# Routed layers in one block: normalisation, gates and routing together, rows scattered in groups of four tiles into a fixed region for each expert

## The reference

```python
# pair 1: relu, no bias, an expert takes its first 320 tokens only
logits = tokens @ gate_w; probs = softmax(logits); expert_idx = argmax(probs)
mask1 = one_hot(expert_idx, E); pos = cumsum(mask1, axis=0) - 1
sec_mask = mask1[:, :, None] * one_hot(pos, 320)
h = relu(einsum('ecd,edf->ecf', expert_input, w1)); expert_output = einsum('ecf,efd->ecd', h, w2)
# pair 3: gelu, biases b1 and b2, no limit
h = gelu(x_flat @ w1[e] + b1[e]); y = h @ w2[e] + b2[e]
out = out + where(expert_idx == e, expert_w, 0)[:, None] * y
```

## Time and profile before

| | us |
|---|---|
| median of 3 runs | 3460.03 (3453.24 to 3462.03) |
| the profiled execution's own time | 3466.94 |
| its span in the profile | 3465.3 |
| TensorE busy | 2923.5 (84%) |
| POOL busy | 1298.7 (37%) |

### The profile page before, as it was taken

The page is one execution under the profiler, slowest core; times in us unless marked ns, Lnnn a source line. Parts: engine busy times, 40 slices in busy tenths (PEclk is TensorE's granted clock), DMA queues, the critical chain, the costliest instruction groups (busy, mean ns, idle before and its releaser), DMA issues. The chain is left out here.

```text
span 3465.3 us, 68349 instructions
## 1 busy us (share of the span) xinstructions
PE 2923.5 (84%) x26674; PEld 2032.6 (59%) x26675; DVE 2086.9 (60%) x3094; ACT 1894.2 (55%) x2864; POOL 1298.7 (37%) x941
## 2 busy tenths in 40 slices
PE   6679997735779998979998595979999999988596
PEld 3246665314436666536666595666666666657595
DVE  6968887485768774867783223756444444466222
ACT  3458885282448885548884111656555555456131
POOL 2259996020127885237873212630000000045212
PEclk9979998867889999989998798979999999989698
DMA  4511111100012220022222511011000000042612
GB/s 160 209 54 54 54 56 59 73 0 19 13 43 55 53 53 22 1 48 59 53 50 77 176 36 51 2 31 49 25 25 25 26 25 1 1 102 50 234 36 68
DMA packets 218052, 193.21 MB, mean 56 GB/s; under 512 B 126837, under 2 KB 176865, under 8 KB 216737
## 3 DMA queue, kind: packets, MB, share of 16 engines
q1 hardware_dynamic: 210247, 172.30, 17.2%
q0 software_dynamic: 5280, 14.42, 1.3%
q10 hardware_dynamic: 2233, 2.39, 0.2%
HBM read 112.72 MB, written 39.00 MB: 44 GB/s over the span
## 5 line engine op out<-in xcount | busy, mean ns | idle before, releaser
L2578 POOL TENSOR_TENSOR lta_p_lo<-lta_p,lta_p_hi 128x1024 f16<-128x1024 f32 x256 | 538.9, 2132 | 221.6 <-DVE lta_p_hi L2701 221.6
L2773 ACT ACTIVATE lta_p<-lta_banks,lt_gmax 128x512 f32<-128x512 f32 x512 | 323.7, 682 | 113.0 <-PE lta_banks L2616 108.5
L2684 DVE TENSOR_REDUCE lta_s_ps<-lta_s_ps 128x1 f32<-128x1101 f32 x240 | 314.2, 1309 | 106.8 <-PE lta_s_ps L2595 106.8
L3717 PE MATMUL m_h_ps<-m_x,m_w 128*128 128x512 f16 x1536 | 356.5, 383 | 4.1 <-issue 4.1
L3729 PE MATMUL m_y_ps<-m_w,m_hT 128*128 128x256 f16 x3072 | 355.8, 273 | 2.3 <-DVE m_hT L3887 2.3
L3887 DVE TENSOR_TENSOR m_hT<-m_h,m_hT 128x512 f16<-128x512 f32 x256 | 177.0, 692 | 281.1 <-ACT m_hT L3814 279.4
L3814 ACT ACTIVATE m_h<-m_h_ps,m_h_bias,m_h_scale 128x512 f32<-128x512 f32 x256 | 199.3, 778 | 266.0 <-PE m_h_ps L3717 257.8
L3729 PEld LDWEIGHTS m_y_ps<-m_w,m_hT 128*128 128x128 f16 x3072 | 298.9, 98 | 65.9 <-issue 8.6
L1227 POOL TENSOR_TENSOR c0a_tri_p_lo<-c0a_tri_p,c0a_tri_p_hi 128x1024 f16<-128x1024 f32 (+2 forms) x192 | 285.5, 1524 | 58.5 <-DVE c0a_tri_p_hi L1401 57.8
L3717 PEld LDWEIGHTS m_h_ps<-m_x,m_w 128*128 128x128 f16 x1536 | 151.1, 99 | 163.0 <-issue 10.6
L1476 ACT ACTIVATE c0a_tri_p<-c0a_banks,c_size 128x512 f32<-128x512 f32 (+3 forms) x384 | 208.3, 576 | 45.6 <-PE c0a_banks L1295 34.3
(11 more groups left out here) (758 smaller groups left out, 6574.7 us busy)
## 6 DMA issues: line engine op xcount, KB each, us to landing
m_w<-in_L_ffn_w_dram SPq DMA_DIRECT2D x4, 8192.0 KB, 39.0
m_raw<-in_L_ffn_W_dram SPq DMA_DIRECT2D x16, 1024.0 KB, 6.5
lta_q<-ltb_qT SPq DMA_DIRECT2D x96, 128.0 KB, 2.4
c_side<-in_fside_Bx16xSxS_dram SPq DMA_DIRECT2D x16, 616.0 KB, 4.9
c0a_tri_q<-c_near SPq DMA_DIRECT2D x96, 96.0 KB
c0a_tri_k<-c_mixed SPq DMA_DIRECT2D x93, 96.0 KB
lta_k<-ltb_kT SPq DMA_DIRECT2D x64, 137.6 KB, 2.5
lt_vh<-ltb_v SPq DMA_DIRECT2D x64, 128.0 KB
```

What stands on the lines that cost most here:

```text
L2578: nc.gpsimd.tensor_tensor(p_lo[:, slot, :], p32[:, p32_slot(h, j), :], p_hi[:, slot, :], ALU.subtract).then_inc(rested, 1)
L2684: nc.vector.tensor_reduce(ntop_of(h)[:, n:n + 1], scores(h, n), AX_X, ALU.max, negate=True).then_inc(top_ready, 1)
L2773: nc.scalar.activation(p32[0:rows, slot, c * 512:(c + 1) * 512], t_ps[0:rows, c, :], ACT.Exp, bias=bias, scale=p["gmax"][0:rows, 0:1]).the ...
L3717: last = nc.tensor.matmul(h_ps[:, f % RING, :], w1[:, v, a, c, f * P:(f + 1) * P], x16[:, b, c, n * CHUNK:(n + 1) * CHUNK], start=c == 0 a ...
```

## The change

- One block holds what were `layernorm_stage` and `route_tokens`. It works in four groups of four tiles: normalise two groups, then for each group choose the experts, normalise a later group, and compute the places. PE, ACT and DVE follow the same order by groups.
- A token's row in `sorted_x` no longer depends on how many tokens the other experts have: expert e owns the rows from e times 2048. So a group of tiles can be scattered as soon as it and the groups before it are counted; POOL waits for `slot_ready` once in four tiles. `sorted_x` grows from 2944 rows to 17408 (8 x 2048 + 8 x 128), 17.8 MB each.
- The old dense row is still computed, after the last group, for `sorted_y` and the gather. A new list `row_of` says for each of the 23 tiles at which row of `sorted_x` it begins; SP reads it with `value_load` before each of its loads.
- The zeros: SP's two fills in stage c0p go. Instead POOL issues four transfers of 4352 rows each at the end of its stream in `latent_project`, for `sorted_x0` in batch 0 and for `sorted_x1` in batch 1. They are waited for (`zero_stored`) before the scatter of the routed layer only.

```diff
@@ Env
-        self.sorted_x = [nc.dram_tensor(f"sorted_x{k}", [NT * P, D], F32).ap() for k in range(2)]
+        self.sorted_x = [nc.dram_tensor(f"sorted_x{k}", [SORTED_ROWS, D], F32).ap() for k in range(2)]
@@ stage c0p, sync
-        for rows, kept in zip(env.sorted_x, env.zero_stored):
-            sp.dma_start(rows.rearrange("(j p) d -> p j d", p=P),
-                         env.zero[:].unsqueeze(1).to_broadcast([P, NT, D])).then_inc(kept, 16)
@@ latent_project, gpsimd
         for n in range(LAST + 1):
             affine(n)
             rest(n)
+        rows = env.sorted_x[b].rearrange("(k j p) d -> k p j d", p=P, k=ZERO_FILLS)
+        for k in range(ZERO_FILLS):
+            nc.gpsimd.dma_start(rows[k], env.zero[:].unsqueeze(1).to_broadcast([P, SORTED_ROWS // P // ZERO_FILLS, D])
+                                ).then_inc(env.zero_stored[b], 16)
@@
+SORTED_ROWS = E * T + E * P
+ZERO_FILLS = 4
@@ route_tokens, gpsimd
-        pool.wait_ge(slot_ready, 1)
-        pool.wait_ge(zero_stored, 16)
+        pool.wait_ge(zero_stored, ZERO_FILLS * 16)
         for t in range(TILES):
-            nc.gpsimd.indirect_dma_start(sorted_x, bass.IndirectOffsetOnAxis(ap=slot[:, t:t + 1], axis=0),
+            if t % GROUP == 0:
+                pool.wait_ge(slot_ready, t // GROUP + 1)
+            nc.gpsimd.indirect_dma_start(sorted_x, bass.IndirectOffsetOnAxis(ap=x_slot[:, t:t + 1], axis=0),
                                          xn[:, t, :], None).then_inc(scattered, 16)
@@ tensor
+        for t in range(TILES + 2):
+            if t < TILES:
+                turn(t)
+            if t >= 2:
+                gates(t - 2)
+            if t >= 2 * GROUP and t % GROUP == 0:
+                count(t // GROUP - 2)
+        count(groups - 1)
@@ scalar
+        for t in range(TILES):
+            keep_rows(t)
+            if t > GROUP and t % GROUP == 2:
+                exponentials(t // GROUP - 1)
+        exponentials(groups - 1)
@@ vector
+            ts(base[:, part], best[:, part], float(T), -1.0, ALU.mult, ALU.add)
+            tt(base[:, part], base[:, part], rank[:, part], ALU.add)
+            nc.vector.tensor_copy(x_slot[:, part], base[:, part]).then_inc(slot_ready, 1)
...
+        for t in range(2 * GROUP):
+            normalise(t)
+        for g in range(groups):
+            choose(g)
+            if g + 2 < groups:
+                for t in tiles_of(g + 2):
+                    normalise(t)
+            place_rows(g)
@@ routed_experts, sync
-            sp.dma_start(xs[:, u, :], sorted_x[bass.ds(j * P, P), :]).then_inc(xs_loaded[u], 16)
+            row = sp.value_load(row_of[0:1, bass.ds(j, 1)], min_val=0, max_val=SORTED_ROWS - P)
+            sp.dma_start(xs[:, u, :], sorted_x[bass.ds(row, P), :]).then_inc(xs_loaded[u], 16)
```

More of the change, by code:

```diff
@@ L2923, in load @@
         sp.dma_start(w2[:], w("w2").rearrange("e (c p) d -> p e c d", p=P)).then_inc(weights_loaded, 16)
[L2925 to L2947, removed]
     @block.gpsimd
@@ L2970, in _ @@
     def _(pe):
[L2971 to L2979, removed]
@@ L2980, in _, with turn, gates @@
-        last.then_inc(counted, 1)
+        def turn(t):
+            pe.wait_ge(normed, t + 1)
+            if t >= TURNED:
+                pe.wait_ge(x_evac, t - TURNED + 1)
+            for c in range(DC):
+                last = nc.tensor.transpose(x_ps[:, t % TURNED, c * P:(c + 1) * P], xn[:, t, c * P:(c + 1) * P], env.ident[:])
+            last.then_inc(x_turned, 1)
+        def gates(t):
+            g, q = divmod(t, GROUP)
+            pe.wait_ge(x_evac, t + 1)
+            if t == 0:
+                pe.wait_ge(gate_loaded, 16)
+            if q == 0 and g >= 2:
+                pe.wait_ge(shifted, g - 1)
+            for c in range(DC):
+                last = nc.tensor.matmul(lg_ps[:, g % 2, q * E:(q + 1) * E], xnT[:, c, t * P:(t + 1) * P], gate[:, c, :],
+                                        start=c == 0, stop=c == DC - 1)
+            if q == GROUP - 1:
+                last.then_inc(lg_done, 1)
@@ new lines, in count @@
+        def count(g):
+            bank = place_ps[:, g % 2, :]
+            pe.wait_ge(hot_ready, g + 1)
+            if g == 0:
+                pe.wait_ge(consts, 5)
+            if g >= 2:
+                pe.wait_ge(slot_ready, g - 1)
+            nc.tensor.matmul(bank[:, 0:GROUP * E], upto[:], hot[:, g * GROUP:(g + 1) * GROUP, :].rearrange("p t e -> p (t e)"),
+                             start=True, stop=False)
+            for t in range(g * GROUP):
+                nc.tensor.matmul(of_group(bank), all_ones[:], hot[:, t:t + 1, :].to_broadcast([P, GROUP, E]), start=False, stop=False)
+            for q in range(GROUP - 1):
+                later = GROUP - 1 - q
+                last = nc.tensor.matmul(bank[:, (q + 1) * E:GROUP * E].rearrange("p (t e) -> p t e", e=E), all_ones[:],
+                                        hot[:, g * GROUP + q:g * GROUP + q + 1, :].to_broadcast([P, later, E]),
+                                        start=False, stop=later == 1)
+            last.then_inc(counted, 1)
@@ new lines, in place_rows @@
+        def place_rows(g):
+            part = slice(g * GROUP, (g + 1) * GROUP)
+            dve.wait_ge(hot_ready, g + 1)
+            dve.wait_ge(counted, g + 1)
+            tt(place[:, part], of_group(place_ps[:, g % 2, :]), hot[:, part], ALU.mult)
+            step(nc.vector.tensor_reduce(rank[:, part], place[:, part], AX_X, ALU.add))
+            tt(base[:, part], base[:, part], rank[:, part], ALU.add)
+            nc.vector.tensor_copy(x_slot[:, part], base[:, part]).then_inc(slot_ready, 1)
+            if capacity is not None:
+                ts(fits[:, part], rank[:, part], float(capacity), None, ALU.is_le)
+                tt(weight[:, part], weight[:, part], fits[:, part], ALU.mult)
@@ L3018, in _ @@
+        dve.wait_ge(summed, 1)
+        over_tiles = lambda buf: buf[:].unsqueeze(1).to_broadcast([P, NT, E])
+        ts(whole[:], b_ps[:, 0:E], 1.0 / P, (P - 1.0) / P - 0.5 + 0.5 / P, ALU.mult, ALU.add)
         ts(whole[:], whole[:], ROUND, -ROUND, ALU.add, ALU.add)
         tt(upto_e[:], whole[:].unsqueeze(1).to_broadcast([P, E, E]), lower[:], ALU.mult)
[L3020 to L3022 removed]
@@ L3034, in _ @@
-        tt(ends[:], per[0][:].unsqueeze(1).to_broadcast([P, NT, E]), tile_ids[:].unsqueeze(2).to_broadcast([P, NT, E]), ALU.is_le)
-        step(nc.vector.tensor_reduce(tile_expert[:], ends[:], AX_X, ALU.add))
+        step(nc.vector.tensor_reduce(ends_at[:], upto_e[:], AX_X, ALU.add))
+        tt(begin[:], ends_at[:], whole[:], ALU.subtract)
+        ts(begin[:], begin[:], float(P), -1.0, ALU.mult, ALU.add)
+        tt(cand[:], hot[:], begin[:].unsqueeze(1).to_broadcast([P, TILES, E]), ALU.mult)
@@ new lines, in _ @@
+        step(nc.vector.tensor_reduce(dense[:], cand[:], AX_X, ALU.add))
+        tt(dense[:], dense[:], rank[:], ALU.add)
+        step(nc.vector.tensor_copy(slot[:], dense[:]))
+        tt(ends[:], over_tiles(ends_at), tile_ids[:].unsqueeze(2).to_broadcast([P, NT, E]), ALU.is_le)
+        step(nc.vector.tensor_reduce(tile_expert[:], ends[:], AX_X, ALU.add))
+        tt(passed[:], ends[:], over_tiles(whole), ALU.mult)
+        step(nc.vector.tensor_reduce(tiles_before[:], passed[:], AX_X, ALU.add))
```

124 lines of the change are left out of this document (81 added, 43 removed).

## The result

The changed kernel takes 3544.32 us (median, 3543.07 to 3551.14), the kernel before 3460.23: ratio 1.0251, 95% interval [1.0231, 1.0270], 84 us slower. The profiled execution has a span of 3548.4 us against 3465.3, 83.1 more.

What follows compares the result with a forecast made beforehand. In routing, w2's landing was taken as the bound; at latent_project's end, POOL's fills held by the barrier. Two times 36.1 less 6.8 gave +65.4 us, 3525 us; own range 3502 to 3531, 8 in 10 range 3500 to 3580.

Steps and rivals of the forecast that it cites:

- Does the barrier wait?: End of latent_project: whether the barrier waits for POOL's fills, 0 or 36.1 us a batch; 36.1 taken as likelier.
- the room of 17.0 us: End of latent_project: POOL is done 17.0 us before the stage's last work on DVE, in each batch.
- The size of the fills: End of latent_project: 35.7 MB in all at 349 GB/s, ending 36.1 us a batch behind the stage's last work.
- Rival 2: End of latent_project: POOL's fills are slower than SP's, 19.3 us each, sum +117 us, 3577; chance 0.18.
- The rate by the Trainium skill: POOL's fills: a rival price of 42.9 us for a batch, +45 us in the sum instead of +65.
- The routing: Routed layers: w2 lands last, so the first expert product gains 4.1 us in pair 1, 2.7 in pair 3.
- The fills taken from c0p: Stage c0p: removing SP's two fills was taken as 0, bound 5.0 us gain.
- SP's value_load: Experts' stage: reads before the 23 tile loads are hidden under a tile's products, 0; without cover 30 us.
- Rival 1: End of latent_project: the barrier does not wait and fills run on into latent_attend, 3451 to 3459; chance 0.17.
- Its step that small loads lose no more than half of the rate beside the fills: Start of latent_attend: head 0's first loads at half of 349 GB/s need 3.9 us instead of 2.0.

Runs made afterwards that it cites:

- b_fills4: The kernel before with only the four POOL fills for each batch added at the end of latent_project: 3551.33 us against 3463.49, ratio 1.0255.
- b_fills3: The kernel before with only three POOL fills for each batch added at the end of latent_project: 3516.19 us, ratio 1.0157.
- b_fills1: The kernel before with only one POOL fill for each batch added at the end of latent_project: 3464.12 us, ratio 0.9999.
- a4_no_drain: The changed kernel with POOL's drain left out of the barriers of latent_project and of the small semaphore-clearing block behind it: 3529.46 us, ratio 1.0196.
- a2_sp_late: The changed kernel with the same four fills at the same place and moment, but issued by SP instead of POOL: 3523.1 us, ratio 1.0178.
- c1_split: a1_sp_early with w2 given its own semaphore, waited for by TensorE only ahead of the first w2 product: 3457.84 us, ratio 0.9979.
- d1_act_loads: c1_split with the first two tile loads of each experts' stage issued by ScalarE's queue instead of SP's: 3450.44 us against 3462.79, ratio 0.9966.
- a1_sp_early: The changed kernel with the fills issued by SP at the start of latent_project instead of POOL at its end: 3458.4 us against 3463.49, ratio 0.9985.
- a3_pool_attend: The changed kernel with POOL's four fills moved past the barrier to the start of POOL's stream in latent_attend: 3499.59 us, ratio 1.0102.

## Why the prediction was right, and where it was off

The time lies in the range, 19 us above the forecast of 3525; the sign and the mechanism were the forecast's.

- **Does the barrier wait?** The step that no row decided went the right way. It is shown by b_fills4 and b_fills3 (the next stage begins 0.8 and 0.9 us behind the last landing), by b_fills1 (no cost within the room of 17.0 us), by a4_no_drain (the landing isn't waited for without the drain) and by a2_sp_late (SP's transfers outlive the barrier, POOL's don't). The argument from the two kinds of queue was only an argument when it was written; the runs bear it out.
- **The size of the fills: mis-sized.** The term was 36.1 us a batch, measured are 43.6 and 43.7; SP's first load came 62.3 us behind POOL's last small instruction, not 54. "They end at 964.3 + 53.1" took one stream of 17.83 MB at 349 GB/s. In the changed kernel it is 61.5 us from POOL's last small instruction (967.77) to the landing of the fourth, which was issued at 1012.81 and in this form takes 16.5 us. Of the 8.4 us more (0.9 of them lie in the room, 17.9 us there), some 3 are the rate (332 GB/s: 53.7 us in place of 51.1), the rest is the slow end of the third fill, the pause and the new start between 1008 and 1017. The hold of a fourth fill behind three was not in the sum; b_fills4 less b_fills3 gives its price as 17.6 us, where a quarter of the stream would be 13.3. All of it together is 2 x 7.6 = 15 us of the 19.
- **Rival 2** priced the issue of a fill at 19.3 us; it is 1.76 us (L2262). POOL's transfers are slower than SP's, but by 5% and a pause, and not for the reason that I gave.
- **The rate by the Trainium skill**, "DMA: Bandwidth & Descriptors", Anatomy of one DMA: 2.0 us + bytes / 436 GB/s, by that estimate 42.9 us. The traces don't agree: the fills moved at 328 to 339 GB/s, so the row was nearer.
- **The routing** was forecast at 4.1 and 2.7 us, and measured at 4.2 and 2.8, and w2 is the last to land as said. The first products came 54.3 and 56.8 us behind the issue of w2 (54 to 56 was written). The first scatter came 15.5 us behind that issue, the last 37.6; 14 and 36 to 39 were written. What the forecast didn't have is that the rows come in behind w2 too, on the same queue (c1_split, d1_act_loads); it moved the time by nothing here, since both waits ended together. a1_sp_early has the routing's gain alone, as 5 us of time.
- **The fills taken from c0p** were taken as 0, and were 0: in a1_sp_early the stage is 0.2 us shorter.
- **SP's value_load** at 0: the 23 loads of `sorted_x` keep their pace (170.3 us against 170.0, above).
- **What remains** of the 19 us, some 4, is not shown. The 2.6 us of the first stage's clock belong to the profiled execution, the slowest of its four (3551.14 us); the medians have no trace, and their spread is of that size.
- **Rival 1** would have given 3451 to 3459. That is what a1_sp_early takes, with the same bytes at another place. But it priced fills beside head 0 at 3 us a batch; a3_pool_attend paid 21, for POOL's hold at its own fourth fill and for head 0's loads, and a4_no_drain 9, of them 7 for head 0's first loads. Its step that small loads lose no more than half of the rate beside the fills didn't hold: `lt_vl` could be used only 36 us behind the start of its issue (a3_pool_attend).

## What to carry to other kernels

Before a bulk transfer is put at the end of an engine's stream, ask what the next barrier makes of it: one started by POOL is part of the stage, so bytes over rate must fit into POOL's room there, and one fill more than its queue takes at once holds the engine itself. The same bytes from SP at the start of a long stage without transfers cost nothing that the runs can tell. And when a step is made to end sooner, look at what lands last behind it, and at what stands in that queue: here the 11.6 and 11.8 us that POOL gained were 4.2 and 2.8 at the first product of the two layers, and these became 5.6 and 7.7 once w2 had a semaphore and the row loads a queue of their own.

## What the runs showed of the hardware

- POOL issues three fills of 4352 rows of 1 KB in 5.3 to 5.6 us, and starts the fourth only 45 us behind the first, when the third has landed (0.3 us before) and the DMA engines have gone idle (0 GB/s from 1012 to 1014). Whether the number of transfers or that of rows sets this, no run here shows.
- SP, too, is held by such fills: three took 22 us to issue and the fourth 13.8 (a1_sp_early), but without a pause between them, at 346 GB/s.
- A barrier with POOL's drain is passed 0.7 to 1.0 us behind the landing of POOL's last transfer (changed kernel, b_fills4, b_fills3); with the drain left out it is passed 0.6 us behind the start of POOL's issue, with the transfer in flight (a4_no_drain).
- SP's issue of a small load, 0.6 us before, took up to 2.5 us beside POOL's fourth fill (a4_no_drain), and one of 0.90 us took 15.38 beside the first three (a3_pool_attend).
- On the queue of an 8 MB load, row loads issued 5.7 and 9.6 us ahead of its landing came in behind it; on another queue the same load landed in 5.3 to 5.7 us and passed it (c1_split, d1_act_loads).
